# The division of an attention output on GpSimd instead of VectorE, in a fused Mamba, attention and MoE kernel

## The chip, the cores and the metric

The kernel runs on one core of one Trainium2 chip. The metric is the device time of one execution in microseconds (us), lower is better. Engines: TensorE (PE; its weight loads are PEld), VectorE (DVE), ScalarE (ACT), GpSimd (POOL), and SyncE (SP), which only issues DMAs.

## What is computed

Input `x` is (2, 2048, 256). A two-directional Mamba2 block, then a block with attention and a mixture of 8 experts. The change is in the attention, cut here to what matters:

```python
q, k, v = heads(src @ q_w), heads(src @ k_w), heads(src @ v_w)   # 16 heads of 16
scores = einsum('bhqd,bhkd->bhqk', q, k) / sqrt(16)
scores = scores * (sigmoid(einsum('bhsd,hd->bhs', q, scale_w)) * 2.0)[..., None]
aw = softmax(scores, axis=-1)
out = einsum('bhqk,bhkd->bhqd', aw, v)                           # sequence 2048, batch 2
```

## The kernel before, in words

`build` runs five stages: norms and steps, Mamba, residual and values, attention, gate and routing, experts. Each is a block in which every engine has its own instruction stream; between stages all engines meet at a barrier, and ahead of the gate stage POOL also clears semaphores there.

The attention (`attention`, L1249) works on 32 **units**. A unit is 512 queries of a group of 4 heads of one batch (8 groups, 4 query blocks each). A unit has 16 **steps**, one for each 128 keys. Three things go on in parallel, for different units:

- **maxima** (20 steps ahead of the rest, `LEAD`): PE multiplies queries by keys into one of three `round_psum` banks (L1357), DVE takes the maximum over 512 keys (L1429). Four of these a step, 64 a unit. At the unit's end DVE takes the negated maximum (L1435), POOL splits it into three bf16 parts (L1462, L1465), PE turns these into rows (`turn_rows`, L1365), ACT copies the rows out of the bank (L1407) and SP sends them into the stacked queries, so that the score products subtract the maximum by themselves.
- **scores**: four pairs of products a step, `main` (L1335) and `rest` (L1344), into `score_psum`; ACT takes exponentials, two of 128x1024 a step (L1401).
- **weighing**: four products a step of the values with the exponentials, summed over the 16 steps in `pv_psum` (L1377). A column of ones in the values gives the denominators.

When a unit's sum is done, ACT copies `pv_psum` to `pv_out` (L1413). Two steps later comes **`turn_out`**: PE turns `pv_out` in four pieces of 128x128 into the next of the three `round_psum` banks (L1386). DVE takes the reciprocal of the 16 denominators in each partition (L1444) and makes four products of 128x64 (L1447), which go into `attn` (the tile is named `tokens` in the profile). The bank counts as free when the last of them is done.

The next group's queries and keys are made meanwhile (`project`, `scale`, `multiply`, `high`, `low`: ACT L926, L931, L937, L941 and POOL L949 to L964); they use the `round_psum` banks too and the same engine queues.

`attention_order` (L1205) gives the order of all that, written out as one list of steps, from which each engine takes its own. In a step the list has six pairs of products, among them the four of the maxima (`max0` first, then `max1` with the third pair, `max2` with the fourth, `max3` with the sixth), then the weighing of the step before, then what is due at that step:

```python
plan(u * KT - LEAD + KT - 1, ("negate", u, 0, 0))
plan(u * KT - LEAD + KT + 1, ("turn_rows", u, 0, 0))
plan(u * KT + KT + 2, ("turn_out", u, 0, 0))
```

Banks are dealt in that order, three in turn (L1272 to L1274), and `bank_read` (L1296) says which event frees a bank: the reduction for a maximum, `rows_stored` for `turn_rows`, `divided` for `turn_out`.

Of the kernel before, what the change touches and what calls it, by code (L numbers as in the profile page):

```python
# [13 lines left out]
P = 128  # L14
# [5 lines left out]
CPB = BLK // P  # L20
# [7 lines left out]
AH, HD = 16, 16  # L28
# [66 lines left out]
def heads(ap, n, w):  # L95
    return ap.rearrange("p (h q) -> p h q", h=n, q=w)


def over_last(ap, w):
    return ap.unsqueeze(2).to_broadcast([ap.shape[0], ap.shape[1], w])  # L100
# [741 lines left out]
HG = 4  # L842
NG = AH // HG
KT = SEQ // P
VW = HD + 1
SB = SEQ // BLK
GROUPS = [(b, g) for b in range(BATCH) for g in range(NG)]
# [342 lines left out]
UNITS = [(n, q) for n in range(len(GROUPS)) for q in range(SB)]  # L1190
NU = len(UNITS)
# [57 lines left out]
def attention(nc, sems, ctx, K, S, V, attn):  # L1249
    def sb(name, shape, dt=F32):  # L1250
        return ctx.enter_context(nc.sbuf_tensor(name, shape, dt))

    def ps(name, shape, dt=F32):
        return ctx.enter_context(nc.psum_tensor(name, shape, dt))
# [6 lines left out]
    mrow = sb("max_rows", [HG * MROWS, 2, BLK], BF16)  # L1261
    pvs = sb("pv_out", [P, BLK])
    rden = sb("rden", [P, CPB * HG])
    ebank = [ps(f"score_psum{i}", [P, 2, BLK]) for i in range(2)]
    pv = ps("pv_psum", [P, BLK])
    rbank = [ps(f"round_psum{i}", [P, BLK]) for i in range(3)]
# [6 lines left out]
    bank = {u: rbank[i % 3] for i, u in enumerate(users)}  # L1273
# [17 lines left out]
    out_turned = sems.events("out_turned", range(NU))  # L1291
    denominator = sems.events("denominator_inverse", range(NU))
    divided = sems.events("out_divided", range(NU))
    pool_own = sems.own("attention_pool")

    def bank_read(step):  # L1296
        what, n, j, i = step
        if what == "max":
            return maxed.at(n, j, i)
        if what == "turn_rows":  # L1300
            return rows_stored.at(n)
        if what == "turn_out":
            return divided.at(n)
        return S.raw_in.at(n, 2 * j + i) if what == "project" else S.ez_in.at(n, j)

    def back(u, k, n):
# [3 lines left out]
    with nc.Block() as block:  # L1310
# [81 lines left out]
        @block.scalar  # L1392
        def _(act):
            for step in order:
                what, u, k, i = step
                if what == "rest" and i % 2 == 0:
                    pair = i // 2
                    act.wait_ge(*scored.at(u, k, pair))
                    if (u, k) >= (0, 2):
                        act.wait_ge(*weighed.at(*back(u, k, 2), pair))  # L1400
                    nc.scalar.activation(pt[:, (k * 2 + pair) % 4, :, :], ebank[pair][:, :, :],  # L1401
                                         ACT.Exp).then_inc(*exped.up(u, k, pair))
                if what == "turn_rows":
                    act.wait_ge(*rows_turned.at(u))
                    if u >= 2:
                        act.wait_ge(*max_row[u % 2].at(u - 2, HG - 1))
                    nc.scalar.copy(mrow[:, u % 2, :],  # L1407
                                   bank[step][0:HG * MROWS, 0:BLK // 2].bitcast(BF16)).then_inc(*rows_stored.up(u))
                if what == "weigh" and k == KT - 1:
                    act.wait_ge(*weighed.at(u, k, 1))  # L1410
                    if u:
                        act.wait_ge(*out_turned.at(u - 1))
                    nc.scalar.copy(pvs[:, :], pv[:, :]).then_inc(*pv_out.up(u))  # L1413
                if what in splits:
                    split_on_scalar(nc, act, S, u, k, what, i, bank[step])
                if what in ("high", "low"):
                    split_on_scalar(nc, act, S, u, k, what, i, None)

        @block.vector
        def _(ve):  # L1420
            nc.vector.memset(pv[:, :], 0.0).then_inc(*zero.up(0))
            for step in order:
                what, u, k, i = step
                if what == "max":
                    h, c, keys = max_at(k, i)
                    ve.wait_ge(*summed.at(u, k, i))
                    if u and k == 0 and i == 0:
                        ve.wait_ge(*negated.at(u - 1))
                    nc.vector.tensor_reduce(mx[:, c * HG + h, keys:keys + 1], bank[step][:, :], AX_X,  # L1429
                                            ALU.max).then_inc(*maxed.up(u, k, i))  # L1430
                if what == "negate":
                    ve.wait_ge(*maxed.at(u, KT - 1, CPB - 1))
                    if u:
                        ve.wait_ge(*part_of.at(u - 1, MROWS - 1))
                    nc.vector.tensor_reduce(neg[:, :], mx[:, :, :], AX_X, ALU.max,  # L1435
                                            negate=True).then_inc(*negated.up(u))
                if what == "turn_out":
                    n, q = UNITS[u]
                    b, g = GROUPS[n]
                    o = bank[step][:, :].rearrange("p (n w) -> p n w", w=32)  # L1440
                    ve.wait_ge(*out_turned.at(u))
                    if u:
                        ve.wait_ge(*divided.at(u - 1))
                    nc.vector.reciprocal(rden[:, :].unsqueeze(2), o[:, :, HD:HD + 1]).then_inc(*denominator.up(u))  # L1444
                    ve.wait_ge(*denominator.at(u))
                    for c in range(CPB):
                        v = nc.vector.tensor_tensor(heads(attn[:, b * KT + q * CPB + c, g * HG * HD:(g + 1) * HG * HD],  # L1447
                                                          HG, HD), o[:, c * HG:(c + 1) * HG, 0:HD],
                                                    over_last(rden[:, c * HG:(c + 1) * HG], HD), ALU.mult)
                    v.then_inc(*divided.up(u))  # L1450

        @block.gpsimd
        def _(po):
            for what, u, j, i in order:
                if what == "negate":
                    po.wait_ge(*negated.at(u))
                    if u:
                        po.wait_ge(*rows_turned.at(u - 1))
                    for part in range(MROWS):
                        if part:  # L1460
                            po.wait_ge(*pool_own.last())
                        nc.gpsimd.tensor_copy(mparts[:, :, part], neg[:, :]).then_inc(*part_of.up(u, part))  # L1462
                        if part < MROWS - 1:
                            po.wait_ge(*part_of.at(u, part))
                            nc.gpsimd.tensor_tensor(neg[:, :], neg[:, :], mparts[:, :, part],  # L1465
                                                    ALU.subtract).then_inc(*pool_own.up())
                if what in ("scale", "multiply", "high", "low"):
                    split_on_pool(nc, po, S, u, j, what, True)

# [830 lines left out]
```

## Time and profile before

| | |
|---|---|
| median of 3 runs | 2653.09 us (2647.68 to 2653.75) |
| the profiled execution, its time | 2651.04 us |
| its span in the trace | 2649.2 us |
| PE / DVE / ACT / POOL busy | 92% / 80% / 66% / 32% |
| attention: first maximum to last products of the division | about 820 to 2256 us |
| costliest group on DVE | L1429, the maxima, 2048 x 684 ns |

The page of a profile gives busy time of each engine and the costliest groups of instructions. The trace behind it can be asked for stretches (busy time of each engine between two times), groups of one engine in a stretch, and a timeline. A row of a timeline that merges several instructions has their number behind an x. "Idle before" is the time that an engine stood still ahead of an instruction, and the arrow names what ended it. "issue" there means that the engine waited for nothing that the profile shows.

### The profile page before, as it was taken

How to read it: one execution, taken by the hardware profiler on the slowest of the kernel's cores; microseconds unless marked ns; L12 is line 12 of the kernel's file. 1: busy time of each engine (PE TensorE's matmuls, PEld its weight loads, DVE VectorE, ACT ScalarE, POOL GpSimd, SP SyncE). 2: the span in 40 equal slices, each digit the busy share in tenths (PEclk: the TensorE clock that was granted, in tenths of full speed). 3: DMA queues.
4: the chain of work that ended last, by engine and by line, in shares of the span. 5: the costliest groups of instructions: out<-in, count | busy, mean ns of one | idle time of the engine just before them, and what ended most of it. 6: DMA issues, size and time to landing. Idle time of an engine off the chain costs nothing. (4 is left out here: it accounts for less than half of the span.)

```text
span 2649.2 us, 44963 instructions
## 1 busy us (share of the span) xinstructions
PE 2447.7 (92%) x16296; PEld 1083.2 (41%) x16296; DVE 2128.9 (80%) x4357; ACT 1754.5 (66%) x2263; POOL 858.5 (32%) x991
## 2 busy tenths in 40 slices
PE   6799999999567999999999999999999999786995
PEld 6366666666442222222222222222222222573553
DVE  4577777787664999999999999999999993693885
ACT  2678777777331677777777777777777778312663
POOL 1377777777650111111110110111000000244663
PEclk9899999999876899999999999999999999877997
DMA  2222232222231040403003012030040000215884
GB/s 88 95 81 72 88 100 83 79 84 84 82 114 47 13 61 13 60 14 60 3 13 61 13 33 29 13 61 3 12 61 2 1 2 1 95 57 209 285 288 141
DMA packets 111280, 179.22 MB, mean 68 GB/s; under 512 B 18796, under 2 KB 85764, under 8 KB 105796
## 3 DMA queue, kind: packets, MB, share of 16 engines
q1 hardware_dynamic: 102724, 158.21, 22.5%
q0 software_dynamic: 6016, 15.41, 1.5%
q8 instruction: 129, 2.11, 0.4%
q10 hardware_dynamic: 2320, 2.74, 0.3%
q14 instruction: 91, 0.75, 0.1%
HBM read 149.47 MB, written 31.21 MB: 68 GB/s over the span
## 5 line engine op out<-in xcount | busy, mean ns | idle before, releaser
L1429 DVE TENSOR_REDUCE max_part<-round_psum 128x1 f32<-128x512 f32 x2048 | 1267.2, 684 | 80.4 <-PE round_psum L1357 76.3
L1401 ACT ACTIVATE p_exp<-score_psum 128x1024 f32<-128x1024 f32 x1024 | 996.1, 1022 | 251.0 <-PE score_psum L1344 243.6
L1357 PE MATMUL round_psum<-k_stack,q_stack 64*128 64x512 bf16 x2048 | 724.7, 390 | 25.6 <-DMA k_stack<-qk_rows 12.6
L1335 PE MATMUL score_psum<-q_stack,k_stack 64*128 64x512 bf16 x2048 | 599.5, 379 | 0.9 <-ACT p_exp L1401 0.2
L1344 PE MATMUL score_psum<-q_stack,k_stack 35*128 35x512 bf16 x2048 | 594.9, 378 | 0.0
L1377 PE MATMUL pv_psum<-p_exp,values 128*17 128x512 f32 x4096 | 539.5, 598 | 0.0
L1357 PEld LDWEIGHTS round_psum<-k_stack,q_stack 64*128 64x128 bf16 x2048 | 191.3, 94 | 638.6 <-DVE max_part L1429 535.1
L559 PE MATMUL rot<-tokens_t,w_in 128*128 128x512 f32 x576 | 274.5, 605 | 16.3 <-DVE bc_conv L697 13.3
L1344 PEld LDWEIGHTS score_psum<-q_stack,k_stack 35*128 35x128 bf16 x2048 | 188.8, 94 | 116.3 <-issue 0.8
L1462 POOL CAST max_parts<-max_neg 128x16 bf16<-128x16 f32 x96 | 20.2, 211 | 602.0 <-DVE max_neg L1435 579.6
L1335 PEld LDWEIGHTS score_psum<-q_stack,k_stack 64*128 64x128 bf16 x2048 | 139.5, 94 | 58.6 <-ACT p_exp L1401 26.2
L766 POOL TENSOR_TENSOR decay<-cum_rows_in,scan_cum 128x1024 f32<-128x1024 f32 x64 | 121.4, 1896 | 109.2 <-PE y_psum L588 56.9
L559 PEld LDWEIGHTS rot<-tokens_t,w_in 128*128 128x128 f32 x576 | 104.6, 193 | 109.1 <-issue 87.2
L949 POOL TENSOR_SCALAR q_scale<-q_scale 128x512 f32<-128x512 f32 x16 | 9.9, 618 | 428.0 <-ACT q_scale L931 428.0
L689 DVE SCALAR_TENSOR_TENSOR rot<-conv_in,chan,rot 128x512 f32<-128x512 f32 x160 | 120.6, 754 | 28.1 <-ACT rot L622 24.7
L608 PE MATMUL rows_psum<-w_out,y_gated 128*128 128x256 f32 x512 | 126.3, 389 | 0.0
L1377 PEld LDWEIGHTS pv_psum<-p_exp,values 128*17 128x17 f32 x4096 | 68.0, 95 | 122.9 <-issue 114.3
L656 ACT ACTIVATE decay<-decay 128x1024 f32<-128x1024 f32 x64 | 67.5, 1055 | 59.3 <-POOL decay L766 58.7
L608 PEld LDWEIGHTS rows_psum<-w_out,y_gated 128*128 128x128 f32 x512 | 92.4, 190 | 9.9
L711 DVE TENSOR_TENSOR x_dt<-xt_psum,scan_dt 128x512 f32<-128x512 f32 x64 | 44.0, 687 | 58.8 <-PE xt_psum L572 58.8
L772 POOL TENSOR_TENSOR c_decayed<-c_decayed,c_t 128x512 f32<-128x512 f32 x60 | 76.5, 1274 | 24.2 <-ACT c_t L641 20.4
L777 POOL TENSOR_TENSOR x_w<-x_dt,scan_eto 128x512 f32<-128x512 f32 x64 | 66.7, 1043 | 46.7 <-DVE x_dt L711 46.6
(249 smaller groups left out, 3452.9 us busy)
## 6 DMA issues: line engine op xcount, KB each, us to landing
expert_w<-in_expert_w SPq DMA_DIRECT2D x39, 1028.0 KB, 5.9
cum_rows_in<-cum_rows SPq DMA_DIRECT2D x64, 512.0 KB, 3.9
cum_pairs_in<-cum_rows SPq DMA_DIRECT2D x120, 128.0 KB, 3.8
qk_rows<-qk_parts SPq DMA_DIRECT2D x64, 192.0 KB, 3.1
q_stack<-qk_rows SPq DMA_DIRECT2D x84, 128.0 KB, 8.1
k_stack<-qk_rows SPq DMA_DIRECT2D x84, 128.0 KB, 9.0
token_rows<-tokens SPq DMA_DIRECT2D x16, 512.0 KB, 3.2
x_in<-in_x SPq DMA_DIRECT2D x8, 512.0 KB, 8.7
```

The source lines that it names most:

```text
L559: m = nc.tensor.matmul(bank[n, c][:, :], w_in[:, k, col:col + P], xnT[:, k, span(block_at(n) * BLK, BLK, d)], start=(k == 0), stop=(k == K ...
L608: m = nc.tensor.matmul(rows_bank[:, 0:D], yg[:, two, c, :], w_out[d][:, c, :], start=False, stop=(c == CI - 1), skip_group_check=True)
L656: nc.scalar.activation(M[:, two, :], M[:, two, :], ACT.Abs).then_inc(*act_own.up())
L689: nc.vector.scalar_tensor_tensor(t[:, :], pre[:, c, i:i + BLK], tap(d, c, i), t[:, :], ALU.mult, ALU.add).then_inc(*own.up())
L766: nc.gpsimd.tensor_tensor(heads(M[:, two, :], NH, P), heads(cum[:, q % 2, :], NH, P), over_last(scan_of("cum", d, q), P), ALU.subtract).th ...
L772: nc.gpsimd.tensor_tensor(ceh, ceh, over_mid(CT[:, sl, ch], NH // 2), ALU.mult).then_inc(*c_ready.up(q))
L1335: nc.tensor.matmul(ebank[i // 2][:, i % 2, :], ks[rows, n % 2, plane, k * P:(k + 1) * P], qs[rows, n % 2, plane, q * BLK:(q + 1) * BLK], s ...
L1344: m = nc.tensor.matmul(ebank[i // 2][:, i % 2, :], ks[rows, n % 2, plane, k * P:(k + 1) * P], qs[rows, n % 2, plane, q * BLK:(q + 1) * BLK ...
L1357: nc.tensor.matmul(bank[step][:, :], qs[rows, n % 2, plane, at:at + P], ks[rows, n % 2, plane, keys * BLK:(keys + 1) * BLK], start=True, s ...
L1377: m = nc.tensor.matmul(pv[h * 32:h * 32 + VW, :], V[:, b * KT + k, g * HG + h, :], pt[:, (k * 2 + h // 2) % 4, h % 2, :], start=(k == 0), ...
L1401: nc.scalar.activation(pt[:, (k * 2 + pair) % 4, :, :], ebank[pair][:, :, :], ACT.Exp).then_inc(*exped.up(u, k, pair))
L1429: nc.vector.tensor_reduce(mx[:, c * HG + h, keys:keys + 1], bank[step][:, :], AX_X, ALU.max).then_inc(*maxed.up(u, k, i))
```

## The change

The division moves to POOL. POOL can't take its operand from where PE left it, so ACT first copies the turned output from `round_psum` into `pv_out` (the same tile that was the input of the turning). POOL takes the power -1 of the 16 denominators and makes the four products. The bank is now free when ACT's copy is done (`out_in`), and ACT's next copy of `pv_psum` into `pv_out` waits for `divided` of the unit before instead of `out_turned`.

```diff
@@ attention
+    minus = sb("minus_one", [P, 1])
+    out_in = sems.events("out_stored", range(NU))
+    one = sems.events("minus_one_ready", [0])
@@ bank_read
         if what == "turn_out":
-            return divided.at(n)
+            return out_in.at(n)
@@ scalar
                 if what == "weigh" and k == KT - 1:
                     act.wait_ge(*weighed.at(u, k, 1))
                     if u:
-                        act.wait_ge(*out_turned.at(u - 1))
+                        act.wait_ge(*divided.at(u - 1))
                     nc.scalar.copy(pvs[:, :], pv[:, :]).then_inc(*pv_out.up(u))
+                if what == "turn_out":
+                    act.wait_ge(*out_turned.at(u))
+                    nc.scalar.copy(pvs[:, :], bank[step][:, :]).then_inc(*out_in.up(u))
@@ vector
-                if what == "turn_out":
-                    n, q = UNITS[u]
-                    b, g = GROUPS[n]
-                    o = bank[step][:, :].rearrange("p (n w) -> p n w", w=32)
-                    ve.wait_ge(*out_turned.at(u))
-                    if u:
-                        ve.wait_ge(*divided.at(u - 1))
-                    nc.vector.reciprocal(rden[:, :].unsqueeze(2), o[:, :, HD:HD + 1]).then_inc(*denominator.up(u))
-                    ve.wait_ge(*denominator.at(u))
-                    for c in range(CPB):
-                        v = nc.vector.tensor_tensor(heads(attn[:, b * KT + q * CPB + c, g * HG * HD:(g + 1) * HG * HD], HG, HD),
                                                    o[:, c * HG:(c + 1) * HG, 0:HD],
-                                                    over_last(rden[:, c * HG:(c + 1) * HG], HD), ALU.mult)
-                    v.then_inc(*divided.up(u))
@@ gpsimd
+            nc.gpsimd.memset(minus[:, :], -1.0).then_inc(*one.up(0))
...
+                if what == "turn_out":
+                    n, q = UNITS[u]
+                    b, g = GROUPS[n]
+                    o = pvs[:, :].rearrange("p (n w) -> p n w", w=32)
+                    po.wait_ge(*out_in.at(u))
+                    if u:
+                        po.wait_ge(*divided.at(u - 1))
+                    else:
+                        po.wait_ge(*one.at(0))
+                    nc.gpsimd.tensor_tensor(rden[:, :], o[:, :, HD], minus[:, :].to_broadcast([P, CPB * HG]),
+                                            ALU.pow).then_inc(*denominator.up(u))
+                    po.wait_ge(*denominator.at(u))
+                    for c in range(CPB):
+                        v = nc.gpsimd.tensor_tensor(heads(attn[:, b * KT + q * CPB + c, g * HG * HD:(g + 1) * HG * HD], HG, HD),
                                                    o[:, c * HG:(c + 1) * HG, 0:HD],
+                                                    over_last(rden[:, c * HG:(c + 1) * HG], HD), ALU.mult)
+                    v.then_inc(*divided.up(u))
```

What the order becomes, at three places. In these rows a line number is that of the kernel named, "x27" counts instructions in a row, and the names of semaphores behind "waits" are partly those of earlier stages whose semaphores are used again.

DVE in a unit of the middle of attention, before:

```order
L1444 RECIPROCAL rden<-round_psum 128x16 [waits out_divided,out_turned]
L1447 TENSOR_TENSOR tokens<-round_psum,rden 128x64 [waits denominator_inverse]
L1447 TENSOR_TENSOR tokens<-round_psum,rden 128x64 x3
L1429 TENSOR_REDUCE max_part<-round_psum 128x1 [waits c_decayed_ready] x36
L1435 TENSOR_REDUCE max_neg<-max_part 128x16 [waits rrms_ready,state_decayed]
L1429 TENSOR_REDUCE max_part<-round_psum 128x1 [waits squares_ready,c_decayed_ready]
L1429 TENSOR_REDUCE max_part<-round_psum 128x1 [waits c_decayed_ready] x27
```

and now:

```order
L1441 TENSOR_REDUCE max_neg<-max_part 128x16 [waits rrms_ready,state_decayed]
L1435 TENSOR_REDUCE max_part<-round_psum 128x1 [waits squares_ready,c_decayed_ready]
L1435 TENSOR_REDUCE max_part<-round_psum 128x1 [waits c_decayed_ready] x63
```

The five instructions between the 28th and the 29th maximum of a unit are gone; the 64 maxima follow one another.

ACT at one of the four units whose `low` casts (L941) are due at the same step as `turn_out`, now (before, the rows are the same without L1419):

```order
L1416 COPY pv_out<-pv_psum 128x512 [waits out_divided,weighed]
L1404 ACTIVATE p_exp<-score_psum 128x1024 [waits weighed,scored] x4
L941 CAST qk_parts<-qk_raw 128x512 [waits products_cb] x2
L1419 COPY pv_out<-round_psum 128x512 [waits out_turned]
L1404 ACTIVATE p_exp<-score_psum 128x1024 [waits weighed,scored] x14
L926 COPY qk_raw<-round_psum 128x512 [waits y_summed,x_normed_ready]
```

The copy is behind both casts here; in the other 28 units it is directly behind the step's exponentials.

POOL at the end of attention, now:

```order
L1458 TENSOR_TENSOR max_neg<-max_neg,max_parts 128x16 [waits rrms_ready]
L1455 CAST max_parts<-max_neg 128x16 [waits attention_pool]
L1469 TENSOR_TENSOR rden<-pv_out,minus_one 128x16 [waits out_divided,out_stored]
L1473 TENSOR_TENSOR tokens<-pv_out,rden 128x64 [waits denominator_inverse]
L1473 TENSOR_TENSOR tokens<-pv_out,rden 128x64 x3
L1313 UNCONDITIONAL_BRANCH
L90 ISA [waits barrier_Pool_Activation_PE_DVE_SP_gather]
L90 ISA x5
```

The power and four products of the last unit are now the last work on POOL before the barrier (L90); before, POOL had nothing behind its cast of the last maxima.

## Rows read from the trace of the kernel before

**Rows 1.** Busy time by stretch: stretch, length, PE, PEld, DVE, ACT, POOL, clock, DMA.
```profile
870.00:2209.00 1339.00, 1329.17 (x10243) 393.63 (x10242) 1256.24 (x2161) 1036.39 (x1138) 135.74 (x245) 1.00 0.16 26
```
**Rows 2.** Groups of DVE, 870 to 2209: count | busy us, mean ns | idle before.
```profile
L1429 DVE TENSOR_REDUCE max_part<-round_psum 128x1 f32<-128x512 f32 x1981 | 1226.7, 684 | 71.8 <-PE round_psum L1357 67.8
L1447 DVE TENSOR_TENSOR tokens<-round_psum,rden 128x64 f32<-128x64 f32 x120 | 18.6, 217 | 1.0
```
**Rows 3.** Timeline of PE, an ordinary step: start us, length us, what.
```profile
1591.64 0.39 PE L1357 MATMUL round_psum<-k_stack,q_stack 64*128 64x512 bf16 x1
...
1594.12 0.39 PE L1357 MATMUL round_psum<-k_stack,q_stack 64*128 64x512 bf16 x1
```
**Rows 4.** Timeline of PE, the turning of an output and the step behind it.
```profile
1588.08 0.66 PE L1386 MATMUL round_psum<-const_f,pv_out 128*128 128x128 f32 x4
1588.67 0.39 PE L1357 MATMUL round_psum<-k_stack,q_stack 64*128 64x512 bf16 x1
...
1589.74 0.39 PE L1357 MATMUL round_psum<-k_stack,q_stack 64*128 64x512 bf16 x1 [0.25 <-DVE tokens L1447]
```
**Rows 5.** Timelines of DVE and ACT, the same place.
```profile
1588.77 0.26 DVE L1444 RECIPROCAL rden<-round_psum 128x16 f32<-128x16 f32 x1 [0.26 <-PE round_psum L1386]
...
1589.60 3.75 DVE L1429 TENSOR_REDUCE max_part<-round_psum 128x1 f32<-128x512 f32 x6
...
1589.52 2.10 ACT L1401 ACTIVATE p_exp<-score_psum 128x1024 f32<-128x1024 f32 x2 [1.12 <-PE score_psum L1344]
```
**Rows 6.** Timeline of all engines, the step behind a turning of the maxima's rows.
```profile
1575.71 0.39 PE L1357 MATMUL round_psum<-k_stack,q_stack 64*128 64x512 bf16 x1
...
1575.81 0.57 ACT L1407 COPY max_rows<-round_psum 12x512 bf16<-12x512 bf16 x1
...
1576.44 0.09 PEld L1357 LDWEIGHTS round_psum<-k_stack,q_stack 64*128 64x128 bf16 x1 [0.35 <-ACT max_rows L1407]
...
1578.18 0.39 PE L1357 MATMUL round_psum<-k_stack,q_stack 64*128 64x512 bf16 x1
```
**Rows 7.** Timelines of ACT and PE, a turning of an output beside two casts.
```profile
1675.70 1.14 ACT L941 CAST qk_parts<-qk_raw 128x512 bf16<-128x512 f32 x2
...
1677.15 0.39 PE L1357 MATMUL round_psum<-k_stack,q_stack 64*128 64x512 bf16 x1 [0.25 <-DVE tokens L1447]
...
1679.05 0.39 PE L1357 MATMUL round_psum<-k_stack,q_stack 64*128 64x512 bf16 x1
```
**Rows 8.** Groups of POOL by shape, whole span: powers (first three), product, subtraction.
```profile
L800 POOL TENSOR_TENSOR rrms<-mean_square,minus_half 128x1 f32<-128x1 f32 x64 | 35.1, 549 | 10.3 <-DVE mean_square L748 10.3
...
L1999 POOL TENSOR_TENSOR tile_rstd<-tile_mv,minus_half 128x3 f32<-128x3 f32 x46 | 46.3, 1007 | 72.1 <-DVE tile_mv L2135 72.1
...
L131 POOL TENSOR_TENSOR n_rstd<-n_rstd,minus_half 128x4 f32<-128x4 f32 x8 | 9.5, 1183 | 27.8 <-DVE n_rstd L127 27.8
...
L794 POOL TENSOR_TENSOR y_squares<-y_squares 128x128 f32<-128x128 f32 x64 | 29.3, 458 | 5.0
...
L1465 POOL TENSOR_TENSOR max_neg<-max_neg,max_parts 128x16 f32<-128x16 f32 x64 | 14.0, 219 | 5.1
```
**Rows 9.** Timeline of ACT behind the turning of unit 30's output.
```profile
2225.50 1.02 ACT L1401 ACTIVATE p_exp<-score_psum 128x1024 f32<-128x1024 f32 x1 [0.97 <-PE score_psum L1344]
```
**Rows 10.** Timeline of all engines, the end of attention.
```profile
2253.57 0.59 ACT L1413 COPY pv_out<-pv_psum 128x512 f32<-128x512 f32 x1 [1.14 <-PE pv_psum L1377]
...
2254.91 0.26 DVE L1444 RECIPROCAL rden<-round_psum 128x16 f32<-128x16 f32 x1 [29.04 <-PE round_psum L1386]
2255.20 0.62 DVE L1447 TENSOR_TENSOR tokens<-round_psum,rden 128x64 f32<-128x64 f32 x4
...
2257.49 1.57 PEld L1647 LDWEIGHTS o_t<-const_f,tokens 128*128 128x128 f32 x8 [2.87 <-issue]
```
**Rows 11.** Timelines of POOL and ACT, scaled queries, their first user.
```profile
1722.22 1.27 POOL L955 TENSOR_TENSOR qk_raw<-qk_raw,q_scale 64x512 f32<-64x512 f32 x1
...
1735.56 1.14 ACT L937 CAST qk_parts<-qk_raw 128x512 bf16<-128x512 f32 x2
```

More of the change, by code:

```diff
@@ L1436, in _ @@
                                             negate=True).then_inc(*negated.up(u))
-                if what == "turn_out":
-                    n, q = UNITS[u]
-                    b, g = GROUPS[n]
-                    o = bank[step][:, :].rearrange("p (n w) -> p n w", w=32)
-                    ve.wait_ge(*out_turned.at(u))
-                    if u:
-                        ve.wait_ge(*divided.at(u - 1))
-                    nc.vector.reciprocal(rden[:, :].unsqueeze(2), o[:, :, HD:HD + 1]).then_inc(*denominator.up(u))
-                    ve.wait_ge(*denominator.at(u))
-                    for c in range(CPB):
-                        v = nc.vector.tensor_tensor(heads(attn[:, b * KT + q * CPB + c, g * HG * HD:(g + 1) * HG * HD],
-                                                          HG, HD), o[:, c * HG:(c + 1) * HG, 0:HD],
-                                                    over_last(rden[:, c * HG:(c + 1) * HG], HD), ALU.mult)
-                    v.then_inc(*divided.up(u))
         @block.gpsimd
         def _(po):
+            nc.gpsimd.memset(minus[:, :], -1.0).then_inc(*one.up(0))
             for what, u, j, i in order:
@@ L1466, in _ @@
                                                     ALU.subtract).then_inc(*pool_own.up())
+                if what == "turn_out":
[11 more added lines that the diff above has]
+                    for c in range(CPB):
+                        v = nc.gpsimd.tensor_tensor(heads(attn[:, b * KT + q * CPB + c, g * HG * HD:(g + 1) * HG * HD],
+                                                          HG, HD), o[:, c * HG:(c + 1) * HG, 0:HD],
+                                                    over_last(rden[:, c * HG:(c + 1) * HG], HD), ALU.mult)
+                    v.then_inc(*divided.up(u))
                 if what in ("scale", "multiply", "high", "low"):
```

## The prediction

> **What bounds the kernel now.** I read the busy shares by stretch first. From 870 to 2209 us the kernel is in the part of attention in which scores, weighing and maxima run together; there PE is busy 1329 us of 1339 and VectorE 1256 us (94%), at a granted clock of 1.00 [rows 1]. ScalarE has 1036 us of work (77%), GpSimd 136 us (10%). The groups of VectorE in that stretch say what the 1256 us are: reductions of the running maxima, 684 ns each, and besides them the division that the change takes away [rows 2].
>
> Two engines over 90% can't both be the bound, so I went to the timeline of PE for the period of a step. In an ordinary step the first maximum's product starts at 1591.64 and the next step's at 1594.12: 2.47 us (2.48 as printed; the two ends are rounded) [rows 3]. The reader is to see in the next groups that neither engine alone sets it. The three `round_psum` banks go round: a product may be written when the reduction three places earlier has read its bank, and PE issues in program order, so a bank that comes free late holds up the scores and the weighing behind it too.
>
> In the step after a turning of the output the round is broken. The four turnings run from 1588.08 for 0.66 us, the first product of the next step follows at 1588.67, and the product that needs the turned output's own bank starts at 1589.74, after an idle of 0.25 us that ends with VectorE's last product of the division [rows 4]. The next step's first product is the 1591.64 of rows 3, so that step takes 1591.64 - 1588.67 = **2.97 us** instead of 2.47. VectorE meanwhile waited 0.26 us for the turnings, did the reciprocal at 1588.77, the products, and took its next maximum only at 1589.60 [rows 5]. So the division is on the path, by holding the bank. The 0.58 us by which the turnings delay PE itself stay.
>
> **The change part by part.**
>
> *Mid-attention, what goes.* Each of 32 units loses one reciprocal (0.26 us) and four products (0.62 us together) from VectorE. Thirty of them stand where maxima are still taken; units 30 and 31 come after the last maximum. The bank is now free when ScalarE's copy ends. The kernel has a step built just like that already: the turning of the maxima's rows, whose bank ScalarE also copies out. There the step's first product starts at 1575.71, the copy runs from 1575.81 for 0.57 us, the held-up weight load follows at 1576.44 (0.06 us after the copy's end), and the following step begins at 1578.18: **2.47 us, no loss**, and 1.74 us behind the release [rows 6].
>
> For the turned output: turnings end 1588.08 + 0.66 = 1588.74; hand-over 0.04 (VectorE took 0.03, rows 5); a 128x512 copy on ScalarE takes 0.59 [rows 10], so it ends at 1589.37; release at + 0.06 = 1589.43; next step at + 1.74 = 1591.17. Against 1591.64 that is **0.47 us won per unit**. ScalarE has the room: its next exponential starts at 1589.52 after 1.12 us of idle [rows 5], and the copy lies wholly inside that idle.
>
> *Four units where ScalarE is not free.* In four of the 30, two casts of `qk_parts` stand right ahead of the copy in ScalarE's order. There they start at 1675.70 and take 1.14 us, to 1676.84 [rows 7]. A copy behind them ends between 1677.33 (instructions on ScalarE overlap by 0.1 us) and 1677.43, the release is at 1677.39 to 1677.49, and + 1.74 gives 1679.13 to 1679.23 against 1679.05 now [rows 7]. So these lose about 0.13 us each instead of winning.
>
> Sum: 26 x 0.47 = 12.2 won, 4 x 0.13 = 0.5 lost.
>
> *GpSimd's new work.* Per unit a power of 128x16, and four products of 128x64. The trace of before has no such power. Its powers take 549 ns for 1 column, 1007 for 3, 1183 for 4 [rows 8]. From 1 to 4 the slope is 0.21 us a column, which gives 0.55 + 15 x 0.21 = 3.7 us; from 3 to 4 it is 0.18, which gives 1.18 + 12 x 0.18 = 3.3. I take **3.5 us**. Bounds: 1.18 us (16 columns no dearer than 4) and 16 x 0.549 = 8.8 us (each as dear as one alone). A product: 219 ns at 16 columns and 458 at 128 [rows 8], so by the line between them 0.32 us at 64; four make 1.3 us, together about 5 us a unit.
>
> A rule of the Trainium skill would price the power otherwise. GPSIMD Engine Reference, section 3.1, gives about 2.6 cycles an element for a two-input operation, which for 16 elements is next to nothing over the fixed part; by it the sum would go as in the first rival below. The three power rows disagree with it, since they grow by some 200 ns a column.
>
> In mid-attention the 5 us are hidden: GpSimd is 10% busy there [rows 1]. What waits in its queue behind them is the scaling of the queries (2.6 us) and the splitting of the maxima. The closest case is a unit whose queries are scaled right behind the division in GpSimd's order: GpSimd ended the scaling at 1723.49 (1722.22 + 1.27), ScalarE wanted it at 1735.56 [rows 11]. Begun instead behind a copy that ends near 1723.2, the power, products and scaling end near 1731; only a power above about 8 us would be felt. The splitting of maxima is nine steps (22 us) behind. The extra memset of 128x1 stands before any work on GpSimd and costs nothing.
>
> *Unit 30.* No maxima run beside it, nobody wants its bank, and ScalarE had 0.97 us of idle before its next exponential [rows 9]; a copy of 0.59 costs 0 to 0.1. I take 0.1.
>
> *The last unit.* Nothing covers it: the stage ends when the output is divided, and a barrier of all engines follows. Now: reciprocal at 2254.91, products to 2255.82, so 0.91 us, and the next stage's first weight load at 2257.49 [rows 10]. After: copy 0.59, hand-over 0.08, power 3.5, hand-over 0.08, products 1.3: 5.5 us. **4.6 us lost** (bounds 2.3 and 9.9).
>
> **Sum:** 12.2 - 0.5 - 0.1 - 4.6 = 7.0 us won, 0.26%. Against the profiled execution's 2651.04 that is 2644.0. That execution is 2.05 us below the median of the runs shown (2653.09) and inside their spread (2647.68 to 2653.75); from the median it would be 2646.1. I forecast **2644.5**, a little towards the latter.
>
> **The rivals.**
>
> *The power is cheap.* If a 16-column power costs what a 16-column subtraction does, 0.22 us [rows 8], the last unit loses only 1.3 us and the sum is 10.3: 2640.7, faster by 0.39%. That is the case that the rule of section 3.1 makes. Against it stand the powers of 1, 3 and 4 columns. Chance 0.08.
>
> *The step isn't shortened.* PE could be the bound of that step by itself, the wait for the division merely coinciding with others. Then nothing is won in the middle and 4.7 lost: 2655.7, within the bound of no change. Against it: the 0.25 us of idle on PE that ends with the division [rows 4], and the row-turning step that makes 2.47 with the same round of banks [rows 6]. Chance 0.08.
>
> *ScalarE is late with the copy in all units (slower).* The copy stands in ScalarE's order behind both exponentials of its step. If these end after the turnings, each unit behaves as the four with casts: 30 x 0.13 = 3.9 lost, plus 4.7: 2659.6, slower by 0.32%. It decides from the point where the release slips by 0.47 us, to 1.23 us behind the step's first product. For it: ScalarE is the next busiest engine. Against it: its 1.12 us of idle in exactly this place [rows 5]. Chance 0.05.
>
> *GpSimd blocks VectorE.* If the maxima stood still during each power, 30 x 3.5 us would be added, some 2749; it decides once a unit loses 0.23 us more than now. The reductions average 684 ns in a stretch in which GpSimd works 136 us [rows 1, 2], so the trace shows no such thing. Chance 0.02. SBUF — State Buffer, section "SBUF: two separate sides", of the Trainium skill, limits the exclusive lock of the two engines to VectorE operations with two SBUF inputs or in a two-port mode; the reductions read one operand from PSUM.
>
> **How the numbers follow.** A measurement of this kernel can tell about 0.3% (8 us) from no change. My case has 0.75, and its centre of 7.0 is 1.0 us short of that bound: I give 0.34 of it to faster (a power near 2.5 us, or 0.51 us a unit, is enough) and 0.41 to same. With the cheap power, faster has 0.42. Same: 0.41 + 0.08 + 0.02 for the unforeseen = 0.51. Slower: 0.05 + 0.02 = 0.07. The range of **2638 to 2653** takes in the power's bounds (2642.2 to 2649.8 about the forecast), the cheap power, and 3 us of scatter of the runs; it leaves out the unshortened step and both slower cases, 0.15, and a little of each tail.
>
> **What the profile would show.** Right: no reciprocal or tensor-tensor of the division on VectorE in attention; PE's wait ahead of the bank ends with ScalarE's copy, 0.76 us behind the step's first product; that step takes 2.50 us; the power at 3.5 us; from the last turnings' end to the next stage 7.2 us instead of 2.6. Wrong: a power far from 3.5 us, exponentials that end behind the turnings, or reductions longer than 684 ns beside GpSimd's work.

## The result, and the profile after

| | before | changed |
|---|---|---|
| median of 14 runs each | 2653.62 us | 2644.74 us |
| lowest to highest | 2647.68 to 2659.72 | 2638.78 to 2649.17 |
| profiled execution, span | 2649.2 | 2643.8 |

The ratio is **0.9964** (95% interval 0.9955 to 0.9974): 0.36% faster, 9.6 us by the ratio. Forecast were 2644.5 us and 7.0 us won; the interval of what was won (6.9 to 11.9 us) just holds the 7.0. That the forecast time lies within 0.3 us of the median is luck: the kernel before came out about 2 us above the time from which I subtracted, and the change won more than I had summed, and the two misses cancel.

Busy shares after: PE 93%, VectorE (DVE) 80%, ScalarE (ACT) 67%, GpSimd (POOL) 37%. The stretch that answers to [rows 1], and the groups that answer to [rows 2] and [rows 8]; in the changed kernel the maxima are L1435, the turnings L1389, the copy L1419, the power L1469, the products L1473:

```profile
870.00:2200.00 1330.00, 1325.32 (x10249) 394.05 (x10248) 1236.33 (x2016) 1049.82 (x1168) 255.37 (x400) 0.99 0.16 26
```
```profile
L1435 DVE TENSOR_REDUCE max_part<-round_psum 128x1 f32<-128x512 f32 x1985 | 1229.8, 683 | 92.6 <-PE round_psum L1360 88.4
```
```profile
L1469 POOL TENSOR_TENSOR rden<-pv_out,minus_one 128x16 f32<-128x16 f32 x32 | 92.8, 2901 | 358.5 <-ACT pv_out L1419 356.2 <-issue 2.3
...
L1473 POOL TENSOR_TENSOR tokens<-pv_out,rden 128x64 f32<-128x64 f32 x128 | 33.4, 293 | 2.5
```

GpSimd's work in the stretch has nearly doubled, and a maximum still takes 683 ns (684 before). The power took 2.90 us, where I took 3.5; a product 0.29, where I took 0.32.

**The middle.** The timelines of PE, PE's weight loads, ScalarE and VectorE at the same unit as [rows 4] and [rows 5]:

```profile
1585.56 0.66 PE L1389 MATMUL round_psum<-const_f,pv_out 128*128 128x128 f32 x4
1586.15 0.39 PE L1360 MATMUL round_psum<-k_stack,q_stack 64*128 64x512 bf16 x1
...
1587.34 0.38 PE L1360 MATMUL round_psum<-k_stack,q_stack 64*128 64x512 bf16 x1
...
1588.63 0.39 PE L1360 MATMUL round_psum<-k_stack,q_stack 64*128 64x512 bf16 x1
```
```profile
1586.89 0.09 PEld L1360 LDWEIGHTS round_psum<-k_stack,q_stack 64*128 64x128 bf16 x1 [0.41 <-ACT pv_out L1419]
```
```profile
1586.25 0.58 ACT L1419 COPY pv_out<-round_psum 128x512 f32<-128x512 f32 x1 [0.37 <-PE round_psum L1389]
```
```profile
1586.57 5.65 DVE L1435 TENSOR_REDUCE max_part<-round_psum 128x1 f32<-128x512 f32 x9 [0.57 <-PE round_psum L1360]
```

The reader is to see three things. The copy runs from 1586.25 to 1586.83 and the held-up load follows at 1586.89, 0.74 us behind the step's first product at 1586.15 (0.76 forecast). The next step begins at 1588.63, 1.74 us behind the release, so the step takes 2.48 us instead of 2.97: 0.49 won (0.47 forecast). And VectorE now stands idle for 0.57 us, during the turnings.

The earlier release (1.07 us behind the first product before) is only part of it. The step's fourth product takes the bank of its first, so it waits for VectorE's reduction of the first maximum. Before, VectorE took that maximum at 1589.60 [rows 5], 0.93 us behind its product, because it had the division to do; now 0.42 us behind. The fourth product of the step, before:

```profile
1590.34 0.09 PEld L1357 LDWEIGHTS round_psum<-k_stack,q_stack 64*128 64x128 bf16 x1 [0.27 <-DVE max_part L1429]
```

It starts 0.74 us behind the start of that reduction, and the next step 1.30 us later, at 1591.64. Now the fourth product starts at 1587.34, 0.45 us behind the release, with the next step again 1.30 us (1.29 as printed) later. So the step ends by the later of two waits: release + 0.45 + 1.30, or the first maximum + 0.74 + 1.30. Before, the two gave 2.82 and 2.97 us; the second decided. By this estimate the earlier release alone, with VectorE as late as before, would have won nothing, and VectorE's earlier maximum alone 0.15 of the 0.49. The change takes away both.

**The four units with casts.** At the unit of [rows 7]: ScalarE, then the load that waits, then the next step.

```profile
1672.19 1.14 ACT L941 CAST qk_parts<-qk_raw 128x512 bf16<-128x512 f32 x2
1673.22 0.60 ACT L1419 COPY pv_out<-round_psum 128x512 f32<-128x512 f32 x1
```
```profile
1673.87 0.09 PEld L1360 LDWEIGHTS round_psum<-k_stack,q_stack 64*128 64x128 bf16 x1 [0.97 <-ACT pv_out L1419]
```
```profile
1672.57 0.39 PE L1360 MATMUL round_psum<-k_stack,q_stack 64*128 64x512 bf16 x1
...
1675.61 0.39 PE L1360 MATMUL round_psum<-k_stack,q_stack 64*128 64x512 bf16 x1
```

The copy waits for both casts, PE's load for the copy, and the step takes 3.04 us, 0.07 more than the 2.97 of before. Forecast was 0.13 more. In each of the other 26 units the step got 0.47 to 0.49 us shorter. (In one of these a scale of the next group stands right ahead of the copy, which the order above doesn't say; it costs that step nothing.)

**The end.** It answers to [rows 10]:

```profile
2245.47 0.66 PE L1389 MATMUL round_psum<-const_f,pv_out 128*128 128x128 f32 x4 [0.69 <-ACT pv_out L1416]
2246.17 0.58 ACT L1419 COPY pv_out<-round_psum 128x512 f32<-128x512 f32 x1 [0.75 <-PE round_psum L1389]
2246.83 2.90 POOL L1469 TENSOR_TENSOR rden<-pv_out,minus_one 128x16 f32<-128x16 f32 x1 [25.93 <-ACT pv_out L1419]
2249.81 1.04 POOL L1473 TENSOR_TENSOR tokens<-pv_out,rden 128x64 f32<-128x64 f32 x4
...
2252.58 1.57 PEld L1657 LDWEIGHTS o_t<-const_f,tokens 128*128 128x128 f32 x8 [6.69 <-issue]
```

Copy, power and four products (1.04 us together, since they overlap) stand one behind the other, uncovered, up to the barrier. From the last turnings' start to the next stage's first load 7.11 us pass.

**Balance of the two traces.** I cut each span at VectorE's first maximum, its last negated maximum, and the next stage's first load.

| us | before | changed | |
|---|---|---|---|
| start to first maximum | 821.8 | 825.2 | + 3.4 |
| first maximum to last negated maximum (the middle) | 1387.8 | 1375.6 | - 12.2 |
| last negated maximum to next stage | 47.9 | 51.8 | + 3.9 |
| next stage to the end | 391.7 | 391.2 | - 0.5 |

The first and last stretch hold no changed instruction but GpSimd's memset; in the traces below the first maximum starts between 821.7 and 826.8 us, so the 3.4 are scatter between executions. The stretches that the change touches give 8.3 us won.

### The profile page after: what moved, and what is told of

It is laid out like the page before. It is cut to its first block and busy times, and to the rows that moved or that the text cites. A ratio compares the mean times of both kernels' runs of the same rounds, so it can differ in the third digit from the quotient of the medians.

```text
span 2643.8 us, 44996 instructions
## 1 busy us (share of the span) xinstructions
PE 2446.9 (93%) x16296; PEld 1087.2 (41%) x16296; DVE 2102.7 (80%) x4197; ACT 1769.8 (67%) x2295; POOL 983.8 (37%) x1152
## 5 line engine op out<-in xcount | busy, mean ns | idle before, releaser
L1435 DVE TENSOR_REDUCE max_part<-round_psum 128x1 f32<-128x512 f32 x2048 | 1267.8, 683 | 101.4 <-PE round_psum L1360 97.2
L1360 PE MATMUL round_psum<-k_stack,q_stack 64*128 64x512 bf16 x2048 | 722.2, 390 | 20.4 <-DMA k_stack<-qk_rows 12.7
L1469 POOL TENSOR_TENSOR rden<-pv_out,minus_one 128x16 f32<-128x16 f32 x32 | 92.8, 2901 | 358.5 <-ACT pv_out L1419 356.2
```

Of the source, the lines that this page charges most:

```text
L1360: nc.tensor.matmul(bank[step][:, :], qs[rows, n % 2, plane, at:at + P], ks[rows, n % 2, plane, keys * BLK:(keys + 1) * BLK], start=True, s ...
L1469: nc.gpsimd.tensor_tensor(rden[:, :], o[:, :, HD], minus[:, :].to_broadcast([P, CPB * HG]), ALU.pow).then_inc(*denominator.up(u))
```

## The experiments

Every kernel below starts from the changed one. "Middle" and "end" are the second and third stretch of the balance, taken from the same events in each trace; they agree to about 0.3 us between executions of like kernels, while whole runs scatter by several us. In what follows the changed kernel is "the change".

| run | middle | end | ratio to before (95%) |
|---|---|---|---|
| the change | 1375.6 | 51.8 | 0.9964 (0.9955 to 0.9974) |
| last unit on VectorE | 1375.4 | 48.0 | 0.9948 (0.9934 to 0.9961) |
| and turning one step later | 1373.7 | 47.7 | 0.9934 (0.992 to 0.9947) |
| the same, repeated | 1373.8 | 47.7 | 0.9949 (0.9937 to 0.9961) |
| four products left on VectorE | 1375.9 | 51.8 | 0.9969 (0.9957 to 0.9981) |
| ten products on VectorE | 1415.2 | 51.8 | 1.0115 (1.0101 to 1.013) |
| bank held until divided | 1559.8 | 51.8 | 1.0648 (1.0629 to 1.0668) |
| power twice | 1375.8 | 54.6 | 0.9975 (0.9966 to 0.9985) |
| VectorE divides from the copy | 1398.1 | 48.6 | 1.0038 (1.0024 to 1.0052) |

### The last unit on VectorE

```diff
-                if what == "turn_out":          # scalar and gpsimd
+                if what == "turn_out" and u < NU - 1:
+                if what == "turn_out" and u == NU - 1:   # vector, from the bank, as before
+                    nc.vector.reciprocal(rden[:, :].unsqueeze(2), o[:, :, HD:HD + 1])
...
```

> The change, but the last unit (31) is divided by VectorE straight from its bank, as before. Theory: the middle of attention wins 0.49 us a unit whatever the last unit does, and the changed kernel gives 3.8 us back at its end (last turnings to next stage 7.1 us instead of 3.3). So the end returns to 3.3 us and the time is that of the change less 3.8: about 2641, 0.48% under the kernel before. Rival: the end is hidden by the loads of the next stage (its first weights land 12 us later anyway), and then this run equals the change, 2644.7.

Measured 2642.18 us, ratio 0.9948. The end is back from 51.8 to 48.0, and the middle didn't move. Its end in the timelines of PE, VectorE and the weight loads:

```profile
2241.71 0.66 PE L1391 MATMUL round_psum<-const_f,pv_out 128*128 128x128 f32 x4 [0.69 <-ACT pv_out L1418]
2242.40 0.26 DVE L1452 RECIPROCAL rden<-round_psum 128x16 f32<-128x16 f32 x1 [45.12 <-PE round_psum L1391]
2242.69 0.62 DVE L1455 TENSOR_TENSOR tokens<-round_psum,rden 128x64 f32<-128x64 f32 x4
...
2245.02 0.86 PEld L1673 LDWEIGHTS o_t<-const_f,tokens 128*128 128x128 f32 x8 [2.90 <-issue]
```

From the turnings' start to the next stage 3.31 us pass, instead of 7.11. The end came back by the 3.8 us that were forecast, so nothing hides it: that rival falls. Unit 30 is still divided by GpSimd here, and the end is within 0.1 us of the 47.9 before, so that unit costs at most what I took for it (0.1).

### And the turning one step later

```diff
-        plan(u * KT + KT + 2, ("turn_out", u, 0, 0))
+        plan(u * KT + KT + 3, ("turn_out", u, 0, 0))
```

> As the run before, and the turning of the output is due one step later (KT + 3), where no cast of ScalarE stands ahead of the copy in any unit. Theory: in the four units with casts the change loses 0.07 us where the others win 0.49, so 4 x 0.56 = 2.2 us come back and no wait of a turned output's bank is longer than in the others: about 2638.7. Rival: those four units pay for something else (the step of the casts is full on ScalarE either way), and the time equals that of the run before, about 2641.

Measured 2638.66 us, ratio 0.9934. The middle is 1.7 us shorter than in the run before (2.2 forecast). At the unit shown above, ScalarE now has casts and copy a step apart, and the copy has its usual place, 0.11 us behind the start of the step's first product at 1673.56, so that step takes 2.49 us:

```profile
1670.71 1.14 ACT L941 CAST qk_parts<-qk_raw 128x512 bf16<-128x512 f32 x2
...
1673.67 0.59 ACT L1421 COPY pv_out<-round_psum 128x512 f32<-128x512 f32 x1
```
```profile
1673.56 0.39 PE L1362 MATMUL round_psum<-k_stack,q_stack 64*128 64x512 bf16 x1
...
1676.05 0.39 PE L1362 MATMUL round_psum<-k_stack,q_stack 64*128 64x512 bf16 x1
```

So the four units are the place, as expected. But the expectation that no casts stand ahead of the copy in any unit was wrong: at another unit, which had been free of them, they do now.

```profile
1022.82 0.60 ACT L1421 COPY pv_out<-round_psum 128x512 f32<-128x512 f32 x1
```
```profile
1023.47 0.39 PE L1362 MATMUL round_psum<-k_stack,q_stack 64*128 64x512 bf16 x1 [0.47 <-ACT pv_out L1421]
```

Its step takes 3.04 us (1022.17 to 1025.21), 0.55 more than in the change, and four times 0.55 won less this 0.55 is the 1.7 us measured. This is the best version tried. It was run again:

> The best version so far once more, on another chip or at another time: 0.66% under the kernel before, between 0.5% and 0.8%.

Measured 2640.86 us, ratio 0.9949 (0.9937 to 0.9961). The middle and the end agree with the first time within 0.1 us; the intervals of the two ratios overlap, and what sets the medians apart, on two different chips, isn't shown. The 0.51% lies at the low edge of what was expected. Two measurements say 0.5% to 0.7% faster than before. Against the change their middle and end together are 6.0 us shorter.

### The same work left on VectorE

Is what was won the bank's early release, or VectorE's time? Here the release stays as in the change, and VectorE gets a reciprocal and four products of the old shapes at the old place, on a constant; they are work on top and replace nothing.

```diff
+                if what == "turn_out" and u < NU - 1:     # vector
+                    o = K["ident"].rearrange("p (n w) -> p n w", w=32)
+                    nc.vector.reciprocal(idle[:, 0:CPB * HG].unsqueeze(2), K["ident"][:, 0:CPB * HG].unsqueeze(2))
+                    for c in range(CPB):
+                        nc.vector.tensor_tensor(heads(idle[:, (c + 1) * HG * HD:(c + 2) * HG * HD], HG, HD),
+                                                o[:, 0:HG, 0:HD], over_last(K["ident"][:, c * HG:(c + 1) * HG], HD),
+                                                ALU.mult)
```

> The change, with a reciprocal of 128x16 and four products of 128x64 left on VectorE at the old place, from a constant into a scratch tile (units 0 to 30): the output doesn't use them. The bank is freed by ScalarE as in the change. Bank alone (theory A: only the bank's hold was paid for): no change against the change, 2644.7. Ring of both (theory B, mine): they no longer wait for the turnings, so the next maximum starts about 0.25 us later than in the change, the fourth product of that step waits for it, and the step is 0.24 us longer: 31 x 0.24 = 7.4 us, about 2652. VectorE's time in full (theory C): 0.9 x 31 = 28 us, 2672.

Measured 2647.57 us, ratio 0.9969; the middle grew by 0.2 us and the end by nothing, so the time above the change's 2644.7 lies outside the stretches that were touched. Theory A's number, not mine. VectorE's timeline:

```profile
1587.29 0.24 DVE L1446 RECIPROCAL idle_work<-const_f 128x16 f32<-128x16 f32 x1
1587.45 0.56 DVE L1448 TENSOR_TENSOR idle_work<-const_f 128x64 f32<-128x64 f32 x4
1587.95 4.37 DVE L1436 TENSOR_REDUCE max_part<-round_psum 128x1 f32<-128x512 f32 x7
```

The five instructions wait for nothing, overlap, and take 0.66 us from start to the next maximum, during the turnings. That maximum starts at 1587.95, 0.42 us behind its product at 1587.53, as in the change. My 0.25 us of delay was too much because I gave the work its old 0.9 us. So at this place VectorE has about 0.6 us for nothing. The run doesn't decide for theory A, though: the old division waited for the turnings and made VectorE's next maximum 0.51 us later than now, and this work doesn't make it late at all. Whether a late maximum would count was open, hence the next run.

### More work on VectorE

The same with `range(10)` in place of `range(CPB)`: a reciprocal and ten products.

> As the run with the same work left on VectorE, but ten products instead of four: 1.5 us of work at the place of the old division, where the changed kernel leaves VectorE idle for 0.57 us. Theory (the idle time covers work, what goes beyond it goes into the ring of banks): the next maximum starts 0.79 us later, the fourth product of the step must wait for it, and the step grows by about 0.77 us: 30 x 0.77 = 23 us more than the change, about 2668. Rival (VectorE's time doesn't count at this place at all, since only the bank's hold does): 2644.7, as with four products.

Measured 2685.82 us, ratio 1.0115; the middle grew by 39.5 us. A unit without casts (VectorE, GpSimd, PE):

```profile
1607.27 1.37 DVE L1448 TENSOR_TENSOR idle_work<-const_f 128x64 f32<-128x64 f32 x10
```
```profile
1608.12 3.29 POOL L1477 TENSOR_TENSOR rden<-pv_out,minus_one 128x16 f32<-128x16 f32 x1 [14.76 <-ACT pv_out L1420]
```
```profile
1609.30 0.39 PE L1361 MATMUL round_psum<-k_stack,q_stack 64*128 64x512 bf16 x1 [0.39 <-DVE max_part L1436]
```

The step behind the turning goes from 1607.35 to 1610.60 and has grown by 0.77 us, from 2.48 to 3.25, as forecast. VectorE took its first maximum at 1608.56, 1.21 us behind the product; the fourth product waits for it and starts 0.74 us after that, and the next step 1.30 us later, just as in the kernel before. The bank was free early here. So the rival that VectorE's time doesn't count there falls, and the ring theory stands with the idle time as its allowance.

The 26 units without casts together account for 19.3 of the 39.5 us. The other 20 us, where some 3 were forecast, sit in the four units with casts, where two steps together grew by 5.0 us a unit (3.3 and 1.7). VectorE and GpSimd there:

```profile
1695.24 3.35 DVE L1448 TENSOR_TENSOR idle_work<-const_f 128x64 f32<-128x64 f32 x10
```
```profile
1695.63 2.29 POOL L964 TENSOR_TENSOR qk_parts<-qk_raw,qk_parts 128x512 bf16<-128x512 f32 x2 [7.65 <-ACT qk_parts L941]
1697.89 2.91 POOL L1477 TENSOR_TENSOR rden<-pv_out,minus_one 128x16 f32<-128x16 f32 x1
```

Ten products take 3.35 us here, instead of 1.37. Their times over the whole execution are:

```profile
L1448 DVE TENSOR_TENSOR idle_work<-const_f x310: 157/216/1190, 935.7 to 2243.5; 128x64 f32<-128x64 f32 x155
```

(shortest, median, longest in ns). The ten wait out GpSimd's two subtractions (L964). VectorE's next maximum is late by that, PE stands idle for it for 1.81 us, and comes back slow; the granted clock (the first column behind the busy times) is 0.50 in the next stretch, and 1.00 after it:

```profile
1699.25 0.60 PE L1361 MATMUL round_psum<-k_stack,q_stack 64*128 64x512 bf16 x1 [1.81 <-DVE max_part L1436]
```
```profile
1699.25:1705.30 6.05, 6.05 (x29) 1.12 (x29) 4.39 (x7) 1.93 (x2) 2.59 (x5) 0.50 0.34 95
1705.50:1712.00 6.50, 6.50 (x56) 2.02 (x52) 5.76 (x10) 4.25 (x5) 0.00 (x0) 1.00 0.00 0
```

So of the 5.0 us the wait for GpSimd is about 2 (3.35 less 1.37) and the extra work 0.8. The remaining 2.2 fall where the clock is low, and I put them down to it; no run takes them apart.

### The bank held until the division is done

```diff
         if what == "turn_out":
-            return out_in.at(n)
+            return divided.at(n)
```

> The change, but the bank counts as free only when GpSimd has divided, though nobody reads it any more after the copy. Theory (the bank is the path): the release moves from 0.76 us behind the step's first product by the power and the products, 4.1 us, in 30 units, and by 2.3 us more in the four in which GpSimd splits first: 123 + 9 = 132 us, about 2777. Rival (what was won is VectorE's time): the same 2644.7.

Measured 2828.37 us, ratio 1.0648: 6.5% slower with not one instruction more, 184 us above the change where 132 were expected. PE around the release at one unit, and three stretches there:

```profile
2116.90 0.39 PE L1360 MATMUL round_psum<-k_stack,q_stack 64*128 64x512 bf16 x1
...
2121.76 0.60 PE L1360 MATMUL round_psum<-k_stack,q_stack 64*128 64x512 bf16 x1 [4.03 <-POOL tokens L1473]
...
2123.15 1.91 PE L1380 MATMUL pv_psum<-p_exp,values 128*17 128x512 f32 x8
2124.99 0.60 PE L1360 MATMUL round_psum<-k_stack,q_stack 64*128 64x512 bf16 x1
...
2128.43 0.39 PE L1360 MATMUL round_psum<-k_stack,q_stack 64*128 64x512 bf16 x1
```
```profile
2100.00:2116.00 16.00, 16.00 (x133) 4.79 (x133) 15.81 (x26) 13.25 (x16) 0.43 (x2) 1.00 0.01 2
```
```profile
2121.80:2127.10 5.30, 5.30 (x25) 1.14 (x26) 2.66 (x4) 1.64 (x2) 0.00 (x0) 0.50 0.00 0
2127.20:2130.00 2.80, 2.80 (x28) 0.81 (x28) 2.34 (x5) 2.04 (x3) 0.00 (x0) 1.00 0.00 0
```

The release comes 4.86 us behind the step's first product, 4.12 later than in the change: that term was right to 0.02 us. What I missed is the clock. PE stood idle for 4.03 us, and behind it the same product takes 0.60 us instead of 0.39 and the eight of the weighing 1.91 instead of 1.05; the granted clock is 1.00 ahead of it, 0.50 up to 2127.1 and 1.00 again from 2127.2. 1.00 is 2.4 GHz, so 0.50 is the lower level of 1.2. The step behind the turning takes 8.09 us here and the next 3.44, instead of 2.49 and 2.47: 6.6 more. Over the 26 units without casts the two steps grew by 5.5 to 6.9 us, 6.0 on average, 1.9 more than the release moved, and in the four with casts by 6.9. The 26 x 1.9 = 50 us are nearly all of the missing 52. That the low clock costs them is read from the longer products; no run holds the bank without an idle PE.

### The power twice

```diff
+                    nc.gpsimd.tensor_tensor(spare[:, :], o[:, :, HD], minus[:, :].to_broadcast([P, CPB * HG]), ALU.pow)
                     nc.gpsimd.tensor_tensor(rden[:, :], o[:, :, HD], minus[:, :].to_broadcast([P, CPB * HG]),
```

> The change with the power of every unit taken twice, the first time into a scratch tile. Theory: GpSimd's work in the middle is hidden, only the last unit's second power shows: 2.9 us more than the change, about 2647.6; the maxima on VectorE stay at 684 ns beside it. Rival: GpSimd's work slows VectorE or is waited for in each unit, up to 31 x 2.9 = 90 us more.

Measured 2647.57 us, ratio 0.9975. The end grew by 2.9 us, the middle by 0.2, and a maximum still takes 684 ns. GpSimd's 4 us of work a unit, and even 7, are hidden in the middle and neither slow nor block VectorE's reductions.

### VectorE divides from the copy, one step later

```diff
+        plan(u * KT + KT + 3, ("divide", u, 0, 0))
...
-                if what == "turn_out":          # gpsimd
+                if what == "divide":            # vector, o = pvs instead of the bank
```

> ScalarE's copy frees the bank as in the change, but VectorE divides, from the copy, one step later. No power on GpSimd. Bank alone (theory A): the middle keeps its 0.49 us a unit and the end is some 3 us shorter than in the change: about 2641.6. Ring of both (theory B): the division now delays the first maximum of a full step by about 0.85 us and the step by as much: 30 x 0.85 = 25 us more than the change, 3 us back at the end: about 2667, slower than the kernel before. Theory C (VectorE's time in full, 1.0 us a unit): 2672.

Measured 2664.26 us, ratio 1.0038: slower than the kernel before. The bank is released as early as in the change, yet the middle grew by 22.4 us; the end is 3.2 us shorter. VectorE:

```profile
2158.35 2.48 DVE L1436 TENSOR_REDUCE max_part<-round_psum 128x1 f32<-128x512 f32 x4 [0.58 <-PE round_psum L1361]
2160.76 0.24 DVE L1451 RECIPROCAL rden<-pv_out 128x16 f32<-128x16 f32 x1
2161.03 0.63 DVE L1454 TENSOR_TENSOR tokens<-pv_out,rden 128x64 f32<-128x64 f32 x4
2161.58 19.80 DVE L1436 TENSOR_REDUCE max_part<-round_psum 128x1 f32<-128x512 f32 x32
```

The idle 0.58 us stand one step too early for the division at 2160.76, which finds VectorE fully used and pushes the maxima back. In most units this step takes 3.21 us instead of 2.47, 0.74 more (0.85 forecast), and in the four with casts 0.3 more. One unit lost 3.2 us by itself, which wasn't forecast: there a GpSimd subtraction runs beside the division, and PE stands idle for VectorE. VectorE, then PE:

```profile
1024.91 1.59 DVE L1454 TENSOR_TENSOR tokens<-pv_out,rden 128x64 f32<-128x64 f32 x4
```
```profile
1027.16 0.39 PE L1361 MATMUL round_psum<-k_stack,q_stack 64*128 64x512 bf16 x1 [1.39 <-DVE max_part L1436]
```

So the 2667 that the ring theory gave came out near the measured time with a step that costs less and a unit that costs more. Theory A alone would have given 2641.6 and falls: the same work is free during the turnings and costs 0.74 us in the next step, with the bank free early in both.

## Why the prediction was right, point by point

- **The division was on the path by holding the bank.** Half of the mechanism. That a bank held for longer lengthens the step is shown: by 0.55 us in the four units with casts, where the release comes 0.56 us later, and by 184 us in all with the bank held until the division is done. But the division also made VectorE late for the step's first maximum, and that wait ended last in the kernel before (2.97 us, against 2.82 by the bank alone). It is shown to count with the bank free early: 0.77 us for 0.79 of lateness with ten products, 0.74 in the run that divides from the copy. The prediction named the bank alone. Its number came out because the step it took as a model, that of the row-turning, has the early release and no late maximum. A run with only the bank released early and the maximum as late as before wasn't made; that it would win nothing is an estimate from these rows.
- **0.47 us a unit.** Measured 0.49, the release 0.74 us behind the first product. 26 x 0.49 = 12.7 won and 4 x 0.07 = 0.3 lost leave 12.4, against 12.2 measured for the middle.
- **The row-turning step as a model** carried that term: its 1.74 us from release to next step came out to the printed digit.
- **Four units with casts.** Right in place and sign; the size was 0.07 us instead of 0.13, because ScalarE's copy and casts overlap by 0.1 us, the favourable end of the forecast. Moving the turning by a step took back 1.7 us.
- **The power.** The term was too dear: 2.90 us against 3.5, and the products 1.04 against 1.3. Straight lines through powers of 1, 3 and 4 columns gave 3.3 to 3.7; the 12 columns between 4 and 16 cost 0.14 us each, less than either slope. By the rule of GPSIMD Engine Reference, section 3.1, of the Trainium skill (about 2.6 cycles an element for two inputs) it would, by my estimate, have been about the 0.22 us of a subtraction of 16 columns; the trace doesn't agree, and that case fell.
- **The end.** 3.9 us lost instead of 4.7 (4.6 and the 0.1 of unit 30), from the power's and the products' size, 0.6 and 0.3 less. The balance of the traces, 8.3 us won, lies 1.3 above the 7.0 of the sum: 0.8 of it here, 0.5 in the middle.
- **Hidden in the middle.** Shown by doubling the power.
- **The rivals.** The cheap power, the unshortened step, the late copy and the blocked VectorE didn't occur: the power took 2.90 us, the step 2.48, the copy started 0.10 us behind the step's first product, and VectorE's reductions kept their 683 ns. Blocking does occur for VectorE's products with two SBUF operands (below).
- **Chances.** The centre lay 1 us short of the bound for faster, and the result passed it, by little: 9.6 us by the ratio, with an interval that begins at 6.9, and 8.3 by the traces. The power at 2.9 us alone would not have done it (7.6); the cheaper products and the 0.49 us a unit were needed as well.

## What to carry to other kernels

When work is moved off an engine, ask first which buffer it holds and who waits for that, then where in time the engine is idle. Here the same work of VectorE cost 0.5 us a unit (behind the turnings, with a bank held and the next maximum late), nothing (during the turnings, bank already free) or 0.74 us (a step later), and holding the bank for 4 us more cost 6 us a unit. And look at the last round by itself: what is hidden thirty times stands open at the barrier, so the slow engine may take all units but the last.

## What the runs showed of the hardware that I had not expected

- **Powers on GpSimd** of 1, 3, 4 and 16 columns took 549, 1007, 1183 and 2901 ns. The columns between 4 and 16 cost 0.14 us each, those up to 4 about 0.2. The first three had the exponent -0.5 and the last -1, so no run shows whether the width or the exponent makes that difference.
- **VectorE and GpSimd do block each other, for some operations.** A VectorE product of 128x64 with both operands in SBUF takes 216 ns and up to 1190 ns beside a GpSimd subtraction of 128x512 (1160 ns); the reductions from PSUM kept 683 ns beside everything. By SBUF — State Buffer, section "SBUF: two separate sides", of the Trainium skill, the two engines share a port pair as an exclusive lock, which a VectorE operation with two SBUF inputs needs only against a GpSimd operation that reads SBUF, and whichever starts first has it for its whole instruction. Beside the subtractions this trace agrees. Beside the power it doesn't: the power that starts at 1697.89 takes its usual 2.91 us although products of VectorE run beside it until 1698.59, and none of VectorE's products lasts near as long as a power. The power that starts at 1608.12 amid ten products takes 3.29 us, while the ten still take 1.37. So VectorE never waits out a power, though the power reads SBUF.
- **An idle of some us on PE costs more than itself.** Behind idles of 4.03 and 1.81 us the granted clock was 0.50, the level of 1.2 GHz, for several us, and products took 0.60 us instead of 0.39. Behind the 1.39 us of idle in the run that divides from the copy it was 0.50 too, from 1027.7 to 1031.0. Idles of 0.25 us [rows 4], of 0.47 us (the four units with casts in the change) and one of 0.71 us (the run that divides from the copy) had no such effect: products kept their 0.39. What lies between 0.71 and 1.39 us wasn't tried.
